# First attention of a two-layer network: values and exponential sums gathered by halves of the queries in one PSUM bank, with the causal mask of the maxima added on VectorE

## The chip, the cores and the metric

One of the cores of a Trainium2 chip runs the whole network. The metric is the device time of one execution in microseconds (us). A core has five engines with a queue each: PE (TensorE, matrix multiplication), ACT (ScalarE), DVE (VectorE), POOL (GpSimd) and SP (SyncE, here the issuer of DMAs). They wait for each other by semaphores.

## What is computed

The program is two transformer layers. Only the first attention is touched. For each of 2 batches and 16 heads it computes, over 2048 tokens, two causal softmaxes and their difference on shared values of 32 columns:

```python
A1 = jnp.einsum('bhqd,bhkd->bhqk', Q1, K1) * scaling
A2 = jnp.einsum('bhqd,bhkd->bhqk', Q2, K2) * scaling
A1 = jnp.where(causal, A1, neg_inf)
A2 = jnp.where(causal, A2, neg_inf)
attn = jax.nn.softmax(A1, -1) - lam * jax.nn.softmax(A2, -1)
O = jnp.einsum('bhqk,bhkd->bhqd', attn, V)
```

The kernel keeps apart, for each of the two softmaxes (index `a`), the products of the exponentials with the values and the sums of the exponentials; both are stored, and the stage that follows (`attention0_out`) divides and subtracts.

## The kernel before

`attention0` handles the 32 heads (2 x 16) one after another. A head has 2048 queries in 4 tiles of 512 (`tq`, also called turns), and for tile `tq` the keys come in 4(tq+1) blocks of 128 (`kb`). That gives 40 steps `k` a head (`STEPS`), each with two halves, a = 0 and 1. In the last four steps of a turn, the diagonal ones, only the queries from `left(k)` = 0, 128, 256 or 384 on have keys to see, and all instructions are shortened to them.

What one step does:

- PE `score` (L768): scores, keys on partitions, 512 queries as columns, in bf16 (each number is split in three bf16 parts that are stacked along the contraction, with the negative maxima as three more rows). In a diagonal step a second matmul adds the mask (L772). There are three PSUM buffers `ps_s` (`RING_S`), so half-step n needs the exponential of half-step n-3.
- ACT (L683): the exponential, from `ps_s` to `probs`, a ring of 8 steps.
- PE `values` (L791), once for two steps: four matmuls in f32 with 32 output rows each, one per column strip of the array: step k and step k+1, each with a = 0 and 1, up to 512 columns. The profile counts each as two MATMULs, so eight make a group. Even and odd steps are thus added up in different strips of the one bank `ps_o`.
- POOL (L638): adds the exponentials of the odd step to those of the even one.
- PE `ones` (L809), once for four steps (`QUAD`): four f32 matmuls against ones, for the two added pairs and a = 0 and 1, into the bank `ps_l`.
- At the first turn of a head a matmul with zeros clears each of the two banks (L777).

Behind each turn ACT copies the odd and the even strips of `ps_o` (L655, L656) two steps into the next turn, and `ps_l` (L665) in its fifth step, DVE adds the odd to the even half (L734), and SP stores both results (`store`, two DMAs).

The maxima that the exponentials subtract are found a head ahead: for the next head, 80 products of 128 queries by up to 512 keys (`MAXIMA`; PE L820, three PSUM buffers `ps_m`), reduced by DVE (L708). In 32 of the 80 a block of 128 x 128 lies on the diagonal, and PE adds the mask to it by one more matmul (L823). They are spread over steps 2 to 31 of the head by a rule of proportion (`maxima_at`), 5 to 7 for two steps; steps 32 to 39, 0 and 1 have none. Then `turn_maxima` (L831) transposes the maxima, DVE splits them in three parts, and three DMAs write them into the stack of the next head. The first head's maxima stand alone at the start.

The order on PE is written out by hand in `step`, for every two steps k, k+1: score(k+2, 0), score(k+2, 1), a third of the maxima, score(k+3, 0), values(k), a second third, score(k+3, 1), the last third, and for each k that is a multiple of 4 `ones` of the four steps before. An engine waits in its own order; what stands behind a waiting instruction waits too. Behind a semaphore wait for `max_used`, for instance, stand the scores that ACT needs next.

## Time and profile before

| | us |
|---|---|
| median of 3 runs | 4359.77 |
| lowest, highest | 4359.03, 4366.46 |
| the profiled execution | 4362.48 |
| its span | 4360.6 |

The span runs from the first to the last instruction that the profile shows. The attention's steady part, from the first to the last transposition of maxima (L831), takes 346.5 to 2586.1 us. In the profile PE is the matmul side of TensorE, PEld the loading of weights beside it. A duration of a matmul there is its latency from start to end; matmuls of a stretch overlap, so what one costs is the distance from its start to the start of the next. PEclk is the share of TensorE's full clock (2.4 GHz) that was granted; half of it is 1.2 GHz.

### The profile page before, as it was taken

The numbers are of one execution on the slowest core, as the hardware profiler recorded it, in microseconds if no ns is written. First come the engines' busy times: TensorE is split into PE (matmuls) and PEld (weight loads), VectorE is DVE, ScalarE is ACT, GpSimd is POOL, SyncE is SP. The second block draws the span as 40 slices with busy tenths as digits, with TensorE's granted clock in tenths as the row PEclk, the third lists the DMA queues.
The fourth block names the chain that finished last, engine by engine and source line by source line (L and its number), as shares of the span: only waits on it lengthen the run. The fifth ranks groups of instructions, "written<-read, shape, count | busy, mean of one in ns | idle before, by whom it ended". The sixth has DMA issues, their size and how long they took to land. (4 is left out here: it accounts for less than half of the span.)

```text
span 4360.6 us, 69689 instructions
## 1 busy us (share of the span) xinstructions
PE 3700.6 (85%) x21166; PEld 1647.8 (38%) x21231; DVE 2467.0 (57%) x4628; ACT 1754.4 (40%) x3522; POOL 1706.6 (39%) x1117
## 2 busy tenths in 40 slices
PE   6869999999999999999999996753899678896794
PEld 3322333232323232323233323642455445555462
DVE  4456766575757576767676753767211276666102
ACT  2324665666656566666666663110122141111110
POOL 1313555555555555555555554400344231110203
PEclk9978999999999999999999997855899899996897
DMA  4431111111111111111111103210443200001332
GB/s 156 154 120 33 34 37 33 34 35 35 35 35 35 35 35 35 35 36 34 38 33 38 31 9 96 82 40 0 121 91 76 45 24 4 0 0 39 111 111 87
DMA packets 202326, 224.92 MB, mean 52 GB/s; under 512 B 86673, under 2 KB 162706, under 8 KB 195858
## 3 DMA queue, kind: packets, MB, share of 16 engines
q1 hardware_dynamic: 186642, 195.39, 15.3%
q0 software_dynamic: 15360, 25.44, 3.1%
q8 instruction: 175, 2.87, 0.3%
q14 instruction: 149, 1.22, 0.1%
HBM read 139.12 MB, written 80.87 MB: 50 GB/s over the span
## 5 line engine op out<-in xcount | busy, mean ns | idle before, releaser
L638 POOL TENSOR_TENSOR attention_probs<-attention_probs 128x1024 f32<-128x1024 f32 (+2 forms) x640 | 1228.1, 1921 | 1160.2 <-PE attention_ps_o L791 1160.1
L708 DVE TENSOR_REDUCE attention_chunk_max<-attention_ps_m 128x1 f32<-128x512 f32 (+3 forms) x2560 | 1394.2, 604 | 457.4 <-PE attention_ps_m L823 280.6
L683 ACT ACTIVATE attention_probs<-attention_ps_s 128x512 f32<-128x512 f32 (+3 forms) x2560 | 1199.5, 532 | 826.9 <-PE attention_ps_s L772 459.7
L768 PE MATMUL attention_ps_s<-attention_q_stack,attention_k_stack 99*128 99x512 bf16 (+3 forms) x2560 | 821.6, 354 | 91.1 <-ACT attention_probs L683 70.1
L820 PE MATMUL attention_ps_m<-attention_k_stack,attention_q_stack 96*128 96x512 bf16 (+3 forms) x2560 | 772.5, 357 | 48.7 <-DMA attention_v_head<-v_rows 34.5
L791 PE MATMUL attention_ps_o<-attention_probs,attention_v_head 128*32 128x512 f32 (+3 forms) x5120 | 647.4, 558 | 8.6 <-issue 5.0
L768 PEld LDWEIGHTS attention_ps_s<-attention_q_stack,attention_k_stack 99*128 99x128 bf16 x2560 | 234.0, 98 | 668.4 <-ACT attention_probs L683 466.0
L820 PEld LDWEIGHTS attention_ps_m<-attention_k_stack,attention_q_stack 96*128 96x128 bf16 x2560 | 224.9, 97 | 628.7 <-DVE attention_chunk_max L708 490.2
L809 PE MATMUL attention_ps_l<-attention_probs,consts 128*32 128x512 f32 (+1 forms) x2560 | 352.6, 580 | 9.7 <-POOL attention_probs L638 1.0
L734 DVE TENSOR_TENSOR attention_out_sb<-attention_even_sb,attention_odd_sb 64x512 f32<-64x512 f32 x128 | 115.0, 898 | 296.8 <-ACT attention_even_sb L656 290.9
L823 PE MATMUL attention_ps_m<-mask_q_bf,ident_bf 128*128 128x128 bf16 x1024 | 225.5, 223 | 0.0
L772 PE MATMUL attention_ps_s<-mask_k_bf,ident_bf 128*128 128x128 bf16 x1024 | 225.4, 226 | 0.0
L1602 DVE TENSOR_TENSOR experts_hidT<-experts_ps_b,experts_silu 128x512 f32<-128x512 f32 x64 | 44.3, 692 | 236.4 <-ACT experts_silu L1568 236.4
L791 PEld LDWEIGHTS attention_ps_o<-attention_probs,attention_v_head 128*32 128x32 f32 x5120 | 101.9, 109 | 181.9 <-issue 115.8
L1549 POOL DMA_INDIRECT experts_sum<-experts_y_sb,experts_index x64 | 100.8, 1574 | 143.6 <-ACT experts_y_sb L1576 128.9
L383 POOL TENSOR_TENSOR project_parts<-project_rest,project_parts 128x512 bf16<-128x512 f32 x64 | 73.7, 1157 | 192.5 <-ACT project_parts L368 192.4
L2252 DVE TENSOR_SCALAR experts_hidT<-experts_ps_a 128x512 f32<-128x512 f32 x32 | 22.1, 692 | 212.5 <-PE experts_ps_a L2270 212.5
L1985 PE MATMUL linear_ps_a<-linear_qblk,linear_kc 128*128 128x512 f32 x256 | 125.1, 615 | 12.4 <-DVE linear_qblk L1960 7.6
L1888 POOL TENSOR_TENSOR x<-x,linear_y 128x256 f32 (+1 forms) x32 | 24.7, 773 | 275.2 <-DVE linear_y L1946 275.2
L443 PE MATMUL project_ps_o<-project_hT,project_wqkv 128*128 128x512 f32 x256 | 113.7, 602 | 13.0 <-ACT project_hT L357 13.0
L1638 PE MATMUL experts_ps_y<-experts_w,experts_hidT 128*128 128x256 f32 x512 | 114.7, 382 | 10.4 <-DVE experts_hidT L1602 10.4
L1621 PE MATMUL experts_ps_a<-experts_xT,experts_w 128*128 128x512 f32 x256 | 122.0, 599 | 1.4 <-ACT experts_xT L1571 1.4
(283 smaller groups left out, 4108.8 us busy)
## 6 DMA issues: line engine op xcount, KB each, us to landing
qk_parts<-project_parts SPq DMA_DIRECT2D x64, 384.0 KB, 3.0
heads_out<-attention_out_sb SPq DMA_DIRECT2D x128, 128.0 KB, 2.3
out_heads<-heads_out SPq DMA_DIRECT2D x8, 2048.0 KB, 8.2
experts_w<-in_f_w SPq DMA_DIRECT2D x16, 1024.0 KB, 8.3
attention_q_stack<-qk_parts SPq DMA_DIRECT2D x32, 384.0 KB
attention_k_stack<-qk_parts SPq DMA_DIRECT2D x32, 384.0 KB
experts_w<-in_e_w SPq DMA_DIRECT2D x24, 512.0 KB, 4.8
v_rows<-project_v SPq DMA_DIRECT2D x8, 1024.0 KB, 4.2
```

The lines of the kernel that those rows point to most:

```text
L638: pool.tensor_tensor(probs[:, to, :, lo:], probs[:, to, :, lo:], probs[:, k % RING_P, :, lo:], ALU.add).then_inc(pair_ok, 1)
L683: act.activation(probs[:, k % RING_P, a, left(k):], ps_s[(2 * k + a) % RING_S][:, left(k):], ACT.Exp, scale=float(DH) ** -0.5).then_inc(pr ...
L708: last = dve.tensor_reduce(chunk_max[:, a, jq, c:c + 1], ps_m[m % RING_M][:, 0:width(m)], AX.X, ALU.max)
L734: dve.tensor_tensor(out[:, slot], even[:, slot], odd[:, slot], ALU.add).then_inc(out_ok, 1)
L768: last = pe.matmul(psum[:, lo:], ks[at][0:WITH_MAX, a, kb * P:(kb + 1) * P], qs[at][0:WITH_MAX, a, tq * GROUP + lo:(tq + 1) * GROUP], star ...
L772: last = pe.matmul(psum[:, lo:lo + P], core.ident_bf[:], core.mask_k_bf[:], start=False, stop=True)
L791: last = pe.matmul(ps_o[strip:strip + DV, lo:], vh[at][:, kb + n], probs[:, (k + n) % RING_P, a, lo:], start=tq > 0 and kb == 0, stop=kb = ...
L809: last = pe.matmul(ps_l[strip:strip + DV, left(k):], core.c("ones")[:, 0:DV], probs[:, k % RING_P, a, left(k):], start=tq > 0 and kb == 0, ...
L820: last = pe.matmul(ps_m[m % RING_M][:, 0:w], qs[at][0:STACK, a, jq * P:(jq + 1) * P], ks[at][0:STACK, a, c * GROUP:c * GROUP + w], start=T ...
L823: last = pe.matmul(ps_m[m % RING_M][:, w - P:w], core.ident_bf[:], core.mask_q_bf[:], start=False, stop=True)
L1621: last = pe.matmul(psum[:], w_up[n][now.at][:, k, m * P:(m + 1) * P], xT[now.part][:, k], start=(k == 0), stop=(k == DC - 1))
L1985: last = pe.matmul(ps_a[hg][:, 4 * n:4 * n + 4].rearrange("p h t -> p (h t)"), kc[1 - at][:, hg], qblk[:, hg, 4 * n:4 * n + 4].rearrange(" ...
```

## The change

- The strips of the array are given out anew. Two of the four strips take the even blocks of 128 queries and two the odd ones (`halves`), each for a = 0 and 1. So `values` is called for each step, with four matmuls of up to 256 columns, and all key blocks add up in the same place. `ones` is called for each pair, in the same form, and its sums go to the other half of the same bank. A bank holds 2 x 2 x 128 columns, values and sums; there are two such banks, `ps_o0` and `ps_o1`, used in turn. No clearing is needed, and no adding of halves.
- ACT makes one copy a turn (`take`, L651 of the changed kernel) in place of three, between the two exponentials of the new turn's fourth step; the semaphores `o_taken`, `l_taken` and `out_ok` give way to one, `taken`.
- SP stores a turn by four DMAs in place of two, with runs of 128 queries (512 bytes) in place of 512; the sums have 2 rows a head in memory in place of 4, and the next stage transposes them with the identity matrix in place of `fold`.
- The mask of the maxima leaves PE. DVE handles the 32 diagonal products a head by `tensor_tensor_reduce` (add `mask_wide`, then the maximum), which is built as two instructions, and the other 48 as before.
- The order on PE is rewritten: the first third of the maxima now stands between score(k+2, 0) and score(k+2, 1), the second third between score(k+2, 1) and score(k+3, 0), then values(k), values(k+1) and ones of the pair before in one block, then score(k+3, 1) and the last third.

```diff
             def take(head, turn):
                 slot = turn % RING_O
...
+                act.wait_ge(values_ok, head * N_STEPS + LAST[turn] + 1)
+                act.wait_ge(ones_ok, head * PAIRS + (LAST[turn] + 1) // PAIR + RING_P // PAIR)
+                act.activation(results[:, slot], ps_o[slot][:], ACT.Copy).then_inc(taken, 1)
...
                     w, to = width(m), chunk_max[:, a, jq, c:c + 1]
+                    if c == jq // GT:
+                        wait_apart(dve, max_ok, after * N_MAX + m + 1, core.passed)
+                        last = dve.tensor_tensor_reduce(ps_m[m % RING_M][:, 0:w], ps_m[m % RING_M][:, 0:w],
+                                                        mask_wide[:, GROUP - w:], 1.0, -3.0e38, ALU.add, ALU.max, to)
+                    else:
+                        dve.wait_ge(max_ok, after * N_MAX + m + 1)
+                        last = dve.tensor_reduce(to, ps_m[m % RING_M][:, 0:w], AX.X, ALU.max)
...
+            def strips(k):
+
+                first = left(k) // P
+                for half in range(2):
+                    block = (first - half + 1) // 2
+                    if block < BLOCKS:
+                        for a in range(2):
+                            yield (half * 2 + a) * DV, half, a, block
...
+                for strip, half, a, block in strips(k):
+                    last = pe.matmul(psum[strip:strip + DV, 0, block:], vh[at][:, kb], halves(k, a, half, block),
+                                     start=kb == 0, stop=False, tile_position=(0, strip), skip_group_check=True)
+                last.then_inc(values_ok, 1)
...
                     if more:
                         score(head, at, k + 2, 0)
+                        maxima(after, other, items[:third])
                         score(head, at, k + 2, 1)
-
-                    third = -(-len(items) // 3)
-                    maxima(after, other, items[:third])
-                    if more:
+                        maxima(after, other, items[third:2 * third])
                         score(head, at, k + 3, 0)
...
                     values(head, at, k)
+                    values(head, at, k + 1)
+                    if k > 0:
+                        ones(head, k // PAIR - 1)
+                    elif not is_first(head):
+                        ones(head - 1, PAIRS - 1)
+                    if more:
+                        score(head, at, k + 3, 1)
```

PE before, one pair of steps in the middle of a head (from a score to the first matmul of `ones`; L768 scores, L820 maxima, L823 their mask, L791 values, L809 ones):

```order
L768 MATMUL attention0_ps_s1<-attention0_q_stack0,attention0_k_stack0 128x512 [waits attention0_prob_ok]
L820 MATMUL attention0_ps_m1<-attention0_k_stack1,attention0_q_stack1 128x512 [waits attention0_max_used]
L820 MATMUL attention0_ps_m2<-attention0_k_stack1,attention0_q_stack1 128x256 [waits attention0_max_used]
L823 MATMUL attention0_ps_m2<-mask_q_bf,ident_bf 128x128
L768 MATMUL attention0_ps_s2<-attention0_q_stack0,attention0_k_stack0 128x512 [waits attention0_prob_ok]
L791 MATMUL attention0_ps_o<-attention0_probs,attention0_v_head0 32x512 [waits attention0_prob_ok]
L791 MATMUL attention0_ps_o<-attention0_probs,attention0_v_head0 32x512 x3
L820 MATMUL attention0_ps_m0<-attention0_k_stack1,attention0_q_stack1 128x512 [waits attention0_max_used]
L820 MATMUL attention0_ps_m1<-attention0_k_stack1,attention0_q_stack1 128x512 [waits attention0_max_used]
L768 MATMUL attention0_ps_s0<-attention0_q_stack0,attention0_k_stack0 128x512 [waits attention0_prob_ok]
L820 MATMUL attention0_ps_m2<-attention0_k_stack1,attention0_q_stack1 128x512 [waits attention0_max_used]
L809 MATMUL attention0_ps_l<-attention0_probs,consts 32x512 [waits attention0_l_taken,attention0_pair_ok]
```

PE in the changed kernel, the like place (L741 scores, L791 maxima, L770 values, L781 ones):

```order
L791 MATMUL attention0_ps_m2<-attention0_k_stack1,attention0_q_stack1 128x512 [waits attention0_max_used]
L741 MATMUL attention0_ps_s1<-attention0_q_stack0,attention0_k_stack0 128x512 [waits attention0_prob_ok]
L791 MATMUL attention0_ps_m0<-attention0_k_stack1,attention0_q_stack1 128x384 [waits attention0_max_used]
L791 MATMUL attention0_ps_m1<-attention0_k_stack1,attention0_q_stack1 128x512 [waits attention0_max_used]
L741 MATMUL attention0_ps_s2<-attention0_q_stack0,attention0_k_stack0 128x512 [waits attention0_prob_ok]
L791 MATMUL attention0_ps_m2<-attention0_k_stack1,attention0_q_stack1 128x512 [waits attention0_max_used]
L791 MATMUL attention0_ps_m0<-attention0_k_stack1,attention0_q_stack1 128x512 [waits attention0_max_used]
L741 MATMUL attention0_ps_s0<-attention0_q_stack0,attention0_k_stack0 128x512 [waits attention0_prob_ok]
L770 MATMUL attention0_ps_o1<-attention0_probs,attention0_v_head0 32x256 [waits attention0_prob_ok]
L770 MATMUL attention0_ps_o1<-attention0_probs,attention0_v_head0 32x256 x7
L781 MATMUL attention0_ps_o1<-attention0_probs,consts 32x256 [waits attention0_pair_ok]
L781 MATMUL attention0_ps_o1<-attention0_probs,consts 32x256 x3
```

Values and ones, which stood apart with maxima on both sides, are one block of 12 calls (24 MATMULs in a profile), and four of a pair's five maxima stand ahead of it, in one run that only scores interrupt.

ACT before, the first steps of a new turn (L683 exponentials, L655 and L656 the copies of the values):

```order
L683 ACTIVATE attention_probs<-attention_ps_s 128x512 [waits attention0_ones_ok]
L679 REGISTER_ALU
L683 ACTIVATE attention_probs<-attention_ps_s 128x512 [waits attention0_score_ok]
L653 REGISTER_ALU
L654 ISA [waits attention0_out_ok]
L655 ACTIVATE attention_odd_sb<-attention_ps_o 64x512 [waits attention0_values_ok]
L656 ACTIVATE attention_even_sb<-attention_ps_o 64x512
L679 REGISTER_ALU
L683 ACTIVATE attention_probs<-attention_ps_s 128x512 [waits attention0_score_ok]
```

ACT in the changed kernel, the fourth step of a new turn (L666 exponentials, L651 the copy):

```order
L666 ACTIVATE attention_probs<-attention_ps_s 128x512 [waits attention0_ones_ok]
L662 REGISTER_ALU
L666 ACTIVATE attention_probs<-attention_ps_s 128x512 [waits attention0_score_ok]
L662 REGISTER_ALU
L666 ACTIVATE attention_probs<-attention_ps_s 128x512 [waits attention0_score_ok]
L648 ISA
L649 ISA [waits attention0_stored0]
L650 REGISTER_ALU [waits attention0_values_ok]
L651 ACTIVATE attention_results_sb<-attention_ps_o 128x512 [waits attention0_ones_ok]
L662 REGISTER_ALU
L666 ACTIVATE attention_probs<-attention_ps_s 128x512 [waits attention0_score_ok]
```

The copies stood behind the second exponential of a turn and ahead of the third; the one copy stands behind the seventh.

## Rows read from the trace of the kernel before

**Rows 1.** The page, its parts 1 and 2 (40 equal slices of the span).

```profile
PE 3700.6 (85%) x21166; PEld 1647.8 (38%) x21231; DVE 2467.0 (57%) x4628; ACT 1754.4 (40%) x3522; POOL 1706.6 (39%) x1117
...
PEclk9978999999999999999999997855899899996897
```

**Rows 2.** Uses of one line, L831: one transposition for each of 32 heads.

```profile
L831 PE MATMUL attention_ps_m<-consts,attention_neg_max x32: 284/284/396, 346.5 to 2586.1; 128*32 128x128 f32 x32
```

**Rows 3.** Groups by line, 346.5 to 2586.1 us: name, count, busy us, mean ns.

```profile
L823 PE MATMUL attention_ps_m<-mask_q_bf,ident_bf 128*128 128x128 bf16 x992 | 215.5, 220 | 0.0
L734 DVE TENSOR_TENSOR attention_out_sb<-attention_even_sb,attention_odd_sb 64x512 f32<-64x512 f32 x123 | 111.5, 907 | 231.8 <-ACT attention_even_sb L656 225.8 <-DMA heads_out<-attention_out_sb 5.9
```

**Rows 4.** Timeline, middle of a head: start us, us taken, engine, instruction.

```profile
1971.22 4.46 DVE L708 TENSOR_REDUCE attention_chunk_max<-attention_ps_m 128x1 f32<-128x512 f32 x8
...
1972.55 0.39 PE L820 MATMUL attention_ps_m<-attention_k_stack,attention_q_stack 96*128 96x512 bf16 x1 [0.18 <-DVE attention_chunk_max L708]
...
1973.15 0.23 PE L820 MATMUL attention_ps_m<-attention_k_stack,attention_q_stack 96*128 96x128 bf16 x1
...
1973.22 0.22 PE L823 MATMUL attention_ps_m<-mask_q_bf,ident_bf 128*128 128x128 bf16 x1
...
1973.28 0.76 PE L768 MATMUL attention_ps_s<-attention_q_stack,attention_k_stack 99*128 99x512 bf16 x2
...
1974.57 0.38 PE L768 MATMUL attention_ps_s<-attention_q_stack,attention_k_stack 99*128 99x512 bf16 x1
...
1974.88 1.06 PE L791 MATMUL attention_ps_o<-attention_probs,attention_v_head 128*32 128x512 f32 x8
...
1975.88 0.50 PE L820 MATMUL attention_ps_m<-attention_k_stack,attention_q_stack 96*128 96x512 bf16 x2
...
1976.06 2.36 POOL L638 TENSOR_TENSOR attention_probs<-attention_probs 128x1024 f32<-128x1024 f32 x1 [3.38 <-PE attention_ps_o L791]
...
1976.31 1.62 DVE L708 TENSOR_REDUCE attention_chunk_max<-attention_ps_m 128x1 f32<-128x512 f32 x3 [0.63 <-PE attention_ps_m L820]
```

**Rows 5.** Timeline of PE where one head ends and the next begins.

```profile
1946.87 0.63 PE L791 MATMUL attention_ps_o<-attention_probs,attention_v_head 128*32 128x256 f32 x8
...
1947.88 0.22 PE L772 MATMUL attention_ps_s<-mask_k_bf,ident_bf 128*128 128x128 bf16 x1
1950.44 0.49 PE L768 MATMUL attention_ps_s<-attention_q_stack,attention_k_stack 99*128 99x384 bf16 x1 [2.35 <-issue]
...
1952.38 1.65 PE L791 MATMUL attention_ps_o<-attention_probs,attention_v_head 128*32 128x512 f32 x8 [0.36 <-issue]
```

**Rows 6.** Timeline of ACT at the same place.

```profile
1947.83 1.08 ACT L683 ACTIVATE attention_probs<-attention_ps_s 128x512 f32<-128x512 f32 x2 [2.57 <-PE attention_ps_s L772]
1948.93 0.59 ACT L655 ACTIVATE attention_odd_sb<-attention_ps_o 64x512 f32<-64x512 f32 x1
1949.54 0.59 ACT L656 ACTIVATE attention_even_sb<-attention_ps_o 64x512 f32<-64x512 f32 x1
```

**Rows 7.** Stretches there: us, busy us (count) by engine, PEclk, DMA share, GB/s.

```profile
1946.40:1950.40 4.00, 1.60 (x14) 0.54 (x14) 0.12 (x1) 2.54 (x5) 1.10 (x2) 0.98 0.20 43
1950.40:1953.80 3.40, 3.00 (x16) 1.08 (x17) 0.56 (x1) 1.36 (x5) 0.00 (x0) 0.53 0.32 90
```

**Rows 8.** DVE's groups by shape, whole span.

```profile
L708 DVE TENSOR_REDUCE attention_chunk_max<-attention_ps_m 128x1 f32<-128x512 f32 x1792 | 1150.9, 683 | 219.3 <-PE attention_ps_m L820 168.3 <-PE attention_ps_m L823 42.5
L708 DVE TENSOR_REDUCE attention_chunk_max<-attention_ps_m 128x1 f32<-128x128 f32 x256 | 73.3, 286 | 195.0 <-PE attention_ps_m L823 195.0
L1757 DVE TENSOR_SCALAR project_low<-project_ps_o,project_bias 128x512 f32<-128x512 f32 x32 | 23.8, 745 | 25.5 <-PE project_ps_o L1789 25.5
L1936 DVE TENSOR_TENSOR linear_state<-linear_ps_s,consts 128x512 f32<-128x512 f32 x32 | 22.1, 692 | 48.7 <-PE linear_ps_s L2007 48.7
L1951 DVE TENSOR_SCALAR linear_den<-linear_ps_tok 128x16 f32<-128x16 f32 x32 | 5.3, 165 | 0.0
```

**Rows 9.** A stretch of the later linear attention, columns as in rows 7.

```profile
3622.31:3624.02 1.71, 1.71 (x28) 1.06 (x28) 1.71 (x2) 0.00 (x0) 0.00 (x0) 1.00 0.00 0
```

More of the change, by code:

```diff
@@ L779, in values @@
             def values(head, at, k):
                 turn, tq, kb = STEPS[k]
[L782 removed]
+                psum = ps_o[turn % RING_O]
+                if kb % PAIR == 0:
+                    pe.wait_ge(prob_ok, head * 2 * N_STEPS + 2 * k + 4)
                 if kb == 0:
[L785 to L793 removed]
@@ L794, in values @@
[L794 to L811 removed]
+                    pe.wait_ge(taken, head * Q_TILES + turn + 1)
@@ L879, in step @@
                 if after is None:
-                    ones(head, QUADS - 1)
+                    ones(head, PAIRS - 1)
             run(pe, step)
```

174 lines of the change are left out of this document (57 added, 117 removed).

## The prediction

> **What bounds the kernel now.** First the busy shares and the slices [rows 1]: PE is the engine with most work. Then one line that runs once a head [rows 2]: from 346.5 to 2586.1 us there are 31 heads, so a head takes 2239.6 / 31 = 72.25 us. That period is what the change touches.
>
> A PE duration is a latency, not a price, so I price by distances between starts [rows 4]. A mask matmul lasts 0.22 us, but starts at 1973.22 with the next start at 1973.28: it costs 0.06. A group of eight values matmuls starts at 1974.88, and the next matmul at 1975.88: 1.00 us, of which 4 x 512 columns at 2.4 GHz are 0.85. The score ahead of it started at 1974.57 and has 0.21 us of columns, so 0.10 goes in front of the group too. A change from full-array to strip matmuls and back thus costs 0.10 + 0.15 = about 0.24 us a group.
>
> By such prices PE's work a head is: scores and maxima 34,816 columns each, 14.8 us each with a few ns a matmul; 64 masks 3.8; values 16 x 0.85 + 4 x 0.43 = 15.4; ones 10 x 0.85 = 8.5; 30 changes 7.2; two clearings and the transposition about 0.6. Sum 65.1 us. The other 7.2 us of the period are PE's waits and slow clock, and two places hold nearly all of it.
>
> The first is the seam between heads [rows 5, 6]. After 1947.88 PE issues nothing until 1950.44, 2.6 us, since the score that stands next needs an exponential that ACT runs behind two copies (1948.93 and 1949.54). Right behind that hole the granted clock is 0.53 for 3.4 us [rows 7], that is mostly the 1.2 GHz level, where before it was 0.98. This costs about 1.7 us. From the last group of values of one head to the second of the next, holes and slow clock come to some 3.9 us of the 7.2.
>
> The second is where DVE falls behind with the maxima: reduces of 512 columns back to back, eight in 4.46 us, and PE issuing one product per 0.60 us (1972.55, 1973.15), waiting for DVE [rows 4]. Sevens of maxima in two steps occur twice a head; such places sum to about 2.6 us. Short waits in the steps that have no maxima make the rest.
>
> **The change, part by part, in us a head.** *Removed from PE's work.* 32 masks x 0.06 = 1.9. Twenty blocks in place of thirty groups: 10 x 0.24 = 2.4. Ones in the last two steps of a turn need half the columns they did: 4 x 0.21 = 0.85. Clearings 0.45. Together -5.6. The columns of values don't change: four strips of 512 for two steps became twice four strips of 256. Between the six quarters of a block I take nothing, since within a group the trace shows the 0.85 of columns and only one 0.15 beside it [rows 4]; the bound above is 0.03 for each of four more joints in 20 blocks, +2.4.
>
> *The seam.* The copies leave the place where PE waits for them. What stays is ACT's own chain: from the end of the last block six scores (1.2 us of PE) go with exponentials of 512, 384 and 384 columns; by the delay of 0.4 from a matmul to its reader and about 0.5 and 0.4 us an exponential, the first block of the new head starts 2.1 us later. That leaves 0.8 us of waits in short pieces, and 0.5 for the last exponential of the old head and POOL's sum. No hole is left like the one ahead of the slow clock, so I take the clock to stay up. Seam: 3.9 becomes 1.4, -2.5.
>
> *Steps without maxima.* Before, ones stood between two scores and filled the time of an exponential in every other pair. Now nothing stands there: a score, 0.4 to its exponential, 0.6 until the third score behind it may start, 1.0 in all, against 0.65 of scores. 0.2 to 0.4 in each of four pairs, +0.4 net.
>
> *DVE's price.* A diagonal maximum is now two instructions. The main one has a row near it, an addition from PSUM of 512 columns, 692 ns against 683 for a reduce [rows 8]. For the second, a column of result, the bound below is a reduce's fixed share: 683 at 512 columns and 286 at 128 leave about 0.15 of duration at none, and as back-to-back reduces start 0.60 apart with 0.68 of duration, 0.07 of spacing. The bound above is 0.165, the whole duration of a 16-column operation, and 0.06 for operands (745 against 683). So a diagonal one costs 0.08 to 0.23 more; a gain is excluded, as the columns are the same and an instruction comes on top. I take 0.12, nearer the lower row, since small operations overlap. On DVE: +3.8, and -4 x 0.9 for the additions of halves that go [rows 3]: level.
>
> *PE's wait for DVE.* This is the term that decides. The chain by rows 4: product to reduce 0.43 (1975.88 to 1976.31), reduce to reduce 0.60, and from a reduce's start to the product that gets its buffer 0.73 (1971.22 + 0.60 = 1971.82, the product at 1972.55). In the new order a usual pair puts on PE, from 0: score, m1, m2, score, m3, m4 (which would start at 1.15), score, then the block of 1.5, score, m5. The m5 of the pair before started at -0.22; its reduce starts at 0.20, that of m1 at 0.80, and m4 can start at 0.80 + 0.73 = 1.53. So PE waits 0.4 us at m4, and 0.06 at m3; behind m4 stand the score that ACT needs and the block. Later DVE is idle through the end of the block. In the old order the values group (1.1 us) lay between the second and third product, and gave DVE the time. For the 15 pairs with maxima: thirteen at 0.1 to 0.8 (mostly 0.5), and the two sevens at 1.2, come to 8.9, against 2.6 now: +6.3. The dearer diagonal ones (0.12 where the chain was followed with 0.085) add 0.4.
>
> *Others.* Four stores for two a turn lie on SP and the DMA queues, with 0.2 to 0.3 DMA share at most there [rows 7]: nothing. POOL's addition (2.36, rows 4) must end within one pair's time instead of two; pairs take 3.4 and more with maxima, 2.6 to 2.8 without, and a block reaches its ones 0.9 after its start, so this is hidden, with 0.3 counted at the seam. The first head's maxima stand alone and are DVE's: 32 x 0.12 = +4 once.
>
> **Sum.** -5.6 - 2.5 + 0.4 + 6.3 + 0.4 = -1.0 a head; 31 heads -31, +4 at the start: -27. Profiled execution 4362.5 - 27 = 4335.5; the median of the runs is 2.7 lower, so 4333.
>
> **Rivals.** *DVE's waits are small.* If bursts of products cost half of what the chain says, +6.3 becomes +2: 4.3 a head, -133 more, 4200. For it: before, PE waits little in most pairs. Against it: 0.73 and 0.60 are measured, and the order leaves only three buffers for five products. Chance 0.17.
>
> *Slower by the price on DVE.* If the pair of instructions costs over 0.22 more than a reduce, the waits grow by about 1 us a head for each 0.1. The place is m1 to m4 in every pair. At 0.30 it is +1.9 a head against my 0.12: +57, 4390. The deciding point is near 0.20. Chance 0.15.
>
> *Slower by the clock.* If the remaining waits at the seam still bring a slow stretch, its 1.7 us a head comes back: +52, 4386. For it: most slices of PEclk show 9 in place of 10 [rows 1], so slow stretches recur. Against it: behind 1.0 us waits elsewhere [rows 4] the clock stayed up. Chance 0.15.
>
> *Slower by the issue of small matmuls.* A block has 24 matmuls and as many weight loads in 1.3 us, 0.054 us each. The densest stretch of the trace has 28 in 1.71, 0.061 each, of which some began earlier [rows 9]; a run of 24 there takes about 1.6. If PE can't issue faster, blocks are 0.2 to 0.3 longer, 20 x 0.25 = +5 a head, minus what it hides of DVE's wait: about +110, 4445. The Trainium skill, "TensorE: Matmul & The Clock Gate", section "Wait — 56ns, not 53.3ns?", says that without hardware decoding the sequencer spends about 62 ns on each MATMUL, which binds below that. By this estimate a block of 24 would take 1.49, +0.2 x 20 = 4 a head. That section also gives a 25 ns floor, by which nothing is lost. The eight of a values group within 0.85 don't test it. Chance 0.08.
>
> **How the numbers follow.** Forecast case 0.43, at 4333 with 4290 to 4370 of its own; the last 0.02 is anything else. What this kernel's measurement can tell from no change is about 0.2%, 9 us. The forecast case gives 0.31 faster, 0.09 same, 0.03 slower; small waits 0.17 faster; the two at 4390 give 0.25 slower and 0.05 same; issue 0.08 slower. Faster 0.49, same 0.14, slower 0.37. The range leaves out half of each outer case: 4200 to 4430.
>
> **What would show it.** L831's first and last start should give 71.2 us a head. Each pair should show a wait of PE for DVE of about 0.4 at the fourth maximum, blocks of 24 matmuls 1.3 to 1.5 long, DVE's two instructions with 0.12 more spacing than a reduce, no 2.6 us hole at the seam and PEclk 1.00 through it. The prediction is wrong if the joints within a block cost time, if the clock drops in new places where DVE's waits have thinned PE's work, or if the second DVE instruction waits for the first to drain.

## The result, and the profile of the changed kernel

| | before | changed |
|---|---|---|
| median, us | 4359.4 (4 runs) | 4482.78 (4 runs) |
| lowest, highest | 4355.14, 4366.46 | 4474.97, 4493.79 |
| profiled execution, its span | 4362.48, 4360.6 | 4480.47, 4478.3 |

The ratio is 1.0283, 95% interval 1.0257 to 1.0309: the change costs 123 us, 2.8%. The forecast was 4333, with 4200 to 4430 as its range; the time lies above both, and the sign was wrong.

The period of a head is read where it was read before [rows 2], by the line that runs once a head:

```profile
L798 PE MATMUL attention_ps_m<-consts,attention_neg_max x32: 275/275/397, 352.1 to 2707.8; 128*32 128x128 f32 x32
```

A head takes (2707.8 - 352.1) / 31 = 75.99 us, where it took 72.25 and 71.2 was forecast. That is 116 of the 118 us between the two profiled executions. So the whole loss lies in the attention's steady part. The page's first part agrees: PE is busy for less time than before [rows 1], in a longer span.

```profile
PE 3670.1 (82%) x27309; PEld 1875.8 (42%) x27311; DVE 2402.8 (54%) x5524; ACT 1663.4 (37%) x3266; POOL 1704.2 (38%) x1117
```

PE therefore waits more. For whom is in its list of waits (352 to 2707 us: what waited for what, us in total, times, longest); the like list of the kernel before stands first.

```profile
PE attention_ps_s L768 <- ACT attention_probs L683: 63.5, 114, 2.5
...
PE attention_ps_m L820 <- DVE attention_chunk_max L708: 9.2, 33, 3.3
PE attention_ps_s L768 <- issue: 7.3, 3, 2.5
```

```profile
PE attention_ps_m L791 <- DVE attention_chunk_max L696: 79.0, 304, 0.4
PE attention_ps_s L741 <- ACT attention_probs L666: 67.9, 77, 5.5
PE attention_ps_m L791 <- DVE attention_chunk_max L692: 37.4, 124, 0.4
PE attention_ps_s L741 <- issue: 28.2, 8, 3.9
```

Two things are new: waits for DVE, 9.2 before and 116.4 now, and single waits for ACT of up to 5.5 us. This list counts only time in which PE is empty; since a matmul's record is longer than its share of the array, short waits hide in it. So for the rest of the text I also use an account by distances between starts: over the whole steady part, the distance from each matmul to the next, less its columns at 2.4 GHz and 5 ns, is put down to the matmul that came late. In us a head:

| kernel | period | scores and maxima, columns | values and ones | late maxima | late scores, under 1.5 us | late scores, over 1.5 us |
|---|---|---|---|---|---|---|
| before | 72.25 | 33.55 | 29.24 | 1.65 | 3.00 | 0.82 |
| changed | 75.99 | 31.69 | 27.39 | 9.37 | 2.08 | 3.12 |

"Values and ones" holds the whole distance from each of these matmuls to the next start. A change from scores to strips is outside these columns (about 0.1 each, 30 before and 20 now), and so are smaller items.

**Late maxima.** Timeline of PE and of DVE in the middle of a head, columns as in [rows 4]:

```profile
1536.76 0.38 PE L741 MATMUL attention_ps_s<-attention_q_stack,attention_k_stack 99*128 99x512 bf16 x1
...
1537.08 0.23 PE L791 MATMUL attention_ps_m<-attention_k_stack,attention_q_stack 96*128 96x128 bf16 x1
1537.73 0.39 PE L791 MATMUL attention_ps_m<-attention_k_stack,attention_q_stack 96*128 96x512 bf16 x1 [0.42 <-DVE attention_chunk_max L692]
...
1538.27 1.07 PE L770 MATMUL attention_ps_o<-attention_probs,attention_v_head 128*32 128x256 f32 x16
1539.16 0.61 PE L781 MATMUL attention_ps_o<-attention_probs,consts 128*32 128x256 f32 x8
1539.70 0.34 PE L741 MATMUL attention_ps_s<-attention_q_stack,attention_k_stack 99*128 99x384 bf16 x1
```

```profile
1536.89 0.72 DVE L692 CUSTOM_DVE_ANT_0 attention_ps_m<-attention_ps_m,attention_mask_wide 128x512 f32<-128x512 f32 x1
1537.53 0.14 DVE L692 DVE_READ_ACCUMULATOR2_ANT attention_chunk_max<- 128x1 f32 x1
1537.53 0.69 DVE L696 TENSOR_REDUCE attention_chunk_max<-attention_ps_m 128x1 f32<-128x512 f32 x1
1538.13 0.29 DVE L692 CUSTOM_DVE_ANT_0 attention_ps_m<-attention_ps_m,attention_mask_wide 128x128 f32<-128x128 f32 x1
1538.34 0.14 DVE L692 DVE_READ_ACCUMULATOR2_ANT attention_chunk_max<- 128x1 f32 x1
1538.34 0.69 DVE L696 TENSOR_REDUCE attention_chunk_max<-attention_ps_m 128x1 f32<-128x512 f32 x1
...
1540.40 0.43 DVE L692 CUSTOM_DVE_ANT_0 attention_ps_m<-attention_ps_m,attention_mask_wide 128x256 f32<-128x256 f32 x1 [1.38 <-PE attention_ps_m L791]
```

The fourth maximum of the pair, at 1537.73, is 0.42 late, and the score and the block stand behind it. Then comes the block, 1.43 us from 1538.27 to 1539.70, and DVE runs dry within it: 1.38 us idle before 1540.40. That is the wait of which the prediction spoke, at its place and of its size. Over all pairs of steps, the eleven with five maxima a head are 0.41 late at the fourth and 0.11 at the third, and the two with seven lose 1.2 each. The same rows show two more things. The read of the accumulator starts together with the next instruction (1537.53 both times), so it takes no time of its own on DVE. From start to start, where DVE is never idle, the median is 0.607 us for a pair of 512 columns and 0.598 for a reduce, 0.207 and 0.198 for 128 columns: 0.01 more (single distances reach 0.65 with both). And a block of 24 matmuls takes 3072 columns at 2.4 GHz, 1.28, and 0.15.

**Late scores.** In 22 of the 31 heads ACT, then PE, stops. SP's row (DMA issues: start, how long the issue took), the ACT copy and the PE behind it:

```profile
1498.03 2.15 SPq L577 DMA_DIRECT2D attention_q_stack<-qk_parts  x3
1500.37 1.97 SPq L577 DMA_DIRECT2D attention_k_stack<-qk_parts  x3
1502.53 0.41 SPq L580 DMA_DIRECT2D attention_v_head<-v_rows  x1
1503.27 20.40 SPq L611 DMA_DIRECT2D heads_out<-attention_results_sb  x1
1523.88 0.60 SPq L613 DMA_DIRECT2D exp_sums<-attention_results_sb  x1
```

```profile
1526.14 0.39 PE L791 MATMUL attention_ps_m<-attention_k_stack,attention_q_stack 96*128 96x512 bf16 x1 [0.26 <-DVE attention_chunk_max L696]
...
1527.33 0.60 ACT L651 ACTIVATE attention_results_sb<-attention_ps_o 128x512 f32<-128x512 f32 x1 [3.69 <-DMA exp_sums<-attention_results_sb]
...
1528.46 0.40 PE L741 MATMUL attention_ps_s<-attention_q_stack,attention_k_stack 99*128 99x512 bf16 x1 [1.94 <-ACT attention_probs L666]
```

The first of the four stores of a turn is issued right behind the next head's seven loads and takes SP 20.40 us; the other three follow from 1523.88. The result buffer of that turn is wanted again two turns later, so ACT's copy waits 3.69 us for it, and behind the copy stand the exponentials. In the eight heads behind a loop's edge (below) the hold was 16.1 to 18.2 us, and only one copy waited, 0.91 us. The copies waited for `exp_sums` 22 times, 92.1 us in all. Before, the same store was held too. SP's row in the kernel before, then ACT's waits for the store behind it (346.5 to 2586.1 us):

```profile
1519.74 20.79 SPq L617 DMA_DIRECT2D heads_out<-attention_out_sb  x1
```

```profile
ACT attention_total_sb L665 <- DMA exp_sums<-attention_total_sb: 9.1, 5, 2.7
```

The held buffers were those of DVE's addition of halves, which waited 5.9 us in all [rows 3] with nothing urgent behind it, and of ACT's copy of the sums, which waited 9.1 us. So ACT was tied to the hold before as well, but it waited only five times.

Behind 20 of the 22 waits of the copy, PE ran at the 1.2 GHz level for 3.4 or 6.8 us; behind a wait for DVE it did not. Stretches, columns as in [rows 7]: behind the stop at 1528.46, and across DVE's waits at 1518 to 1521.5.

```profile
1528.40:1531.90 3.50, 3.44 (x26) 1.20 (x27) 0.00 (x0) 1.48 (x4) 1.06 (x1) 0.54 0.17 39
1518.00:1521.50 3.50, 3.02 (x29) 1.33 (x29) 3.00 (x7) 1.44 (x3) 0.72 (x1) 1.00 0.15 56
```

**The seam.** The hole where one head ends and the next begins [rows 5] is still there, and longer, but only at every third head:

```profile
1574.03 0.22 PE L745 MATMUL attention_ps_s<-mask_k_bf,ident_bf 128*128 128x128 bf16 x1
1577.59 0.50 PE L741 MATMUL attention_ps_s<-attention_q_stack,attention_k_stack 99*128 99x384 bf16 x1 [3.34 <-issue]
```

At the head after it the same instructions run without a stop:

```profile
1651.37 0.39 PE L741 MATMUL attention_ps_s<-attention_q_stack,attention_k_stack 99*128 99x512 bf16 x1
...
1651.88 0.33 PE L741 MATMUL attention_ps_s<-attention_q_stack,attention_k_stack 99*128 99x384 bf16 x1
...
1653.49 0.85 PE L770 MATMUL attention_ps_o<-attention_probs,attention_v_head 128*32 128x256 f32 x14
```

The stretch from the first of the seam's six scores to the first values of the new head takes 2.12 us here, just the 2.1 of the prediction. And the kernel before has the same two kinds, told apart by which head one looks at. An ordinary seam of before:

```profile
1804.40 0.39 PE L768 MATMUL attention_ps_s<-attention_q_stack,attention_k_stack 99*128 99x512 bf16 x1
...
1804.91 0.33 PE L768 MATMUL attention_ps_s<-attention_q_stack,attention_k_stack 99*128 99x384 bf16 x1
...
1807.13 0.28 PE L768 MATMUL attention_ps_s<-attention_q_stack,attention_k_stack 99*128 99x256 bf16 x1 [1.25 <-ACT attention_probs L683]
...
1807.94 1.05 PE L791 MATMUL attention_ps_o<-attention_probs,attention_v_head 128*32 128x512 f32 x8
```

The score at 1804.91 is the one that started at 1950.44 in [rows 5], and nothing holds it. ACT beside it:

```profile
1805.50 0.59 ACT L655 ACTIVATE attention_odd_sb<-attention_ps_o 64x512 f32<-64x512 f32 x1
1806.11 0.59 ACT L656 ACTIVATE attention_even_sb<-attention_ps_o 64x512 f32<-64x512 f32 x1
```

What the two copies cost PE is the 1.25 at 1807.13. Over all seams the stretch takes 3.64 us before and 2.16 now at the 23 ordinary ones, 5.02 and 5.63 at the other 8. The 8 lie three heads apart (637, 860, 1077, 1296, 1514, 1732, 1948 and 2163 us before), and the loop over heads, `run`, has three heads in a round.

### The profile page after: what moved, and what is told of

It is laid out like the page before. It is cut to its first block and busy times, and to the rows that moved or that the text cites. A ratio compares the mean times of both kernels' runs of the same rounds, so it can differ in the third digit from the quotient of the medians.

```text
span 4478.3 us, 84226 instructions
## 1 busy us (share of the span) xinstructions
PE 3670.1 (82%) x27309; PEld 1875.8 (42%) x27311; DVE 2402.8 (54%) x5524; ACT 1663.4 (37%) x3266; POOL 1704.2 (38%) x1117
## 3 DMA queue, kind: packets, MB, share of 16 engines
q14 instruction: 168, 1.38, 0.1%
## 5 line engine op out<-in xcount | busy, mean ns | idle before, releaser
L666 ACT ACTIVATE attention_probs<-attention_ps_s 128x512 f32<-128x512 f32 (+3 forms) x2560 | 1247.9, 536 | 997.6 <-PE attention_ps_s L741 517.8
L696 DVE TENSOR_REDUCE attention_chunk_max<-attention_ps_m 128x1 f32<-128x512 f32 x1536 | 998.9, 685 | 368.2 <-PE attention_ps_m L791 368.2
L791 PE MATMUL attention_ps_m<-attention_k_stack,attention_q_stack 96*128 96x512 bf16 (+3 forms) x2560 | 837.5, 361 | 177.5 <-DVE attention_chunk_max L696 80.7
L741 PE MATMUL attention_ps_s<-attention_q_stack,attention_k_stack 99*128 99x512 bf16 (+3 forms) x2560 | 880.2, 358 | 122.3 <-ACT attention_probs L666 72.7
L692 DVE CUSTOM_DVE_ANT_0 attention_ps_m<-attention_ps_m,attention_mask_wide 128x128 f32<-128x128 f32 (+3 forms) x1024 | 496.9, 498 | 508.6 <-PE attention_ps_m L791 505.5
L770 PE MATMUL attention_ps_o<-attention_probs,attention_v_head 128*32 128x256 f32 (+1 forms) x9728 | 655.1, 374 | 0.4 <-ACT attention_probs L666 0.4
L791 PEld LDWEIGHTS attention_ps_m<-attention_k_stack,attention_q_stack 96*128 96x128 bf16 x2560 | 246.6, 98 | 616.5 <-DVE attention_chunk_max L696 329.1
L741 PEld LDWEIGHTS attention_ps_s<-attention_q_stack,attention_k_stack 99*128 99x128 bf16 x2560 | 248.3, 98 | 546.2 <-ACT attention_probs L666 224.0
L781 PE MATMUL attention_ps_o<-attention_probs,consts 128*32 128x256 f32 (+1 forms) x5120 | 422.3, 368 | 2.4 <-POOL attention_probs L633 1.2
L770 PEld LDWEIGHTS attention_ps_o<-attention_probs,attention_v_head 128*32 128x32 f32 x9728 | 267.0, 111 | 267.7 <-issue 107.6
L781 PEld LDWEIGHTS attention_ps_o<-attention_probs,consts 128*32 128x32 f32 x5120 | 192.2, 112 | 104.4 <-POOL attention_probs L633 33.1
L692 DVE DVE_READ_ACCUMULATOR2_ANT attention_chunk_max<- 128x1 f32 x1024 | 144.6, 141 | 0.0
L651 ACT ACTIVATE attention_results_sb<-attention_ps_o 128x512 f32<-128x512 f32 x128 | 76.4, 597 | 179.3 <-DMA exp_sums<-attention_results_sb 92.1
```

The lines of the kernel that those rows point to most:

```text
L666: act.activation(probs[:, k % RING_P, a, left(k):], ps_s[(2 * k + a) % RING_S][:, left(k):], ACT.Exp, scale=float(DH) ** -0.5).then_inc(pr ...
L692: last = dve.tensor_tensor_reduce(ps_m[m % RING_M][:, 0:w], ps_m[m % RING_M][:, 0:w], mask_wide[:, GROUP - w:], 1.0, -3.0e38, ALU.add, ALU ...
L696: last = dve.tensor_reduce(to, ps_m[m % RING_M][:, 0:w], AX.X, ALU.max)
L741: last = pe.matmul(psum[:, lo:], ks[at][0:WITH_MAX, a, kb * P:(kb + 1) * P], qs[at][0:WITH_MAX, a, tq * GROUP + lo:(tq + 1) * GROUP], star ...
L770: last = pe.matmul(psum[strip:strip + DV, 0, block:], vh[at][:, kb], halves(k, a, half, block), start=kb == 0, stop=False, tile_position=( ...
L781: last = pe.matmul(psum[strip:strip + DV, 1, block:], core.c("ones")[:, 0:DV], halves(k, a, half, block), start=False, stop=kb == GT * (tq ...
```

## Experiments

All are compared with runs of the kernel before on the same chip (4366.34, 4364.31 and 4365.65 us for the three groups of runs below). "Changed" stands for 4482.78, measured where the kernel before took 4359.4; so a difference from it is less sure than a ratio, and by the ratios the gains over the changed kernel would be 5 to 7 us larger. The account by distances between starts, us a head:

| kernel | time | period | values and ones | late maxima | late scores, short | late scores, over 1.5 us |
|---|---|---|---|---|---|---|
| changed | 4482.78 | 75.99 | 27.39 | 9.37 | 2.08 | 3.12 |
| four result buffers | 4386.68 | 73.01 | 26.68 | 9.25 | 1.86 | 1.26 |
| stores ahead of loads | 4383.33 | 72.99 | 26.59 | 9.27 | 1.93 | 1.26 |
| maxima spread | 4372.95 | 72.82 | 27.60 | 3.63 | 2.32 | 5.07 |
| thirds as before | 4415.56 | 73.86 | 27.63 | 5.56 | 2.29 | 4.28 |
| four buffers and spread | 4208.33 | 67.32 | 26.73 | 3.33 | 2.07 | 1.19 |
| that, six heads a round | 4177.61 | 66.38 | 26.54 | 3.29 | 2.18 | 0.43 |
| that of 4208, mask on PE | 4240.21 | 68.35 | 26.74 | 2.32 | 1.76 | 1.71 |

**Four result buffers.** The wait of the copy is taken away by buffers:

```diff
-        results = s.sb("results_sb", [P, RING_O, 2, BLOCKS, P], F32)
+        results = s.sb("results_sb", [P, Q_TILES, 2, BLOCKS, P], F32)
-        stored = [s.sem(f"stored{i}") for i in range(RING_O)]
+        stored = [s.sem(f"stored{i}") for i in range(Q_TILES)]
...
-                act.activation(results[:, slot], ps_o[slot][:], ACT.Copy).then_inc(taken, 1)
+                act.wait_ge(stored[turn], (head + 1) * (STORES * 16))
+                act.activation(results[:, turn], ps_o[turn % RING_O][:], ACT.Copy).then_inc(taken, 1)
```

> The changed kernel with four buffers for a turn's results in place of two, so that a copy on ACT waits for the store of the same turn one head earlier. Theory S (stores): once a head ACT's copy waits 4 us for a store that SP issues late (92 us in 22 waits), PE stands still 2.3 to 4.5 us behind it, and a slow clock follows; this goes: 2.5 to 3 us a head, 75 to 95 us, 4385 to 4410. Rival D (DVE alone): all that matters is PE's wait for DVE, and what the stores hold up is made good later: within 15 us of the changed kernel's 4483.

Measured: 4386.68 us (4379.43 to 4395.21), ratio to before 1.0046 (1.003 to 1.0063), 96 us under the changed kernel. ACT's waits for `exp_sums` are gone from its list, and of the late scores over 1.5 us the eight holes at the loop's edge make up most of what is left. So a term that the prediction put at nothing costs 96 us, 3.0 of every head.

**Stores ahead of loads.** Is it the place of the store in the queue, or are four stores of 512-byte runs too slow? Two buffers again, one edit on SP:

```diff
+                if head is not None and not is_first(head.n):
+                    store(head.n, 0)
                 if later is not None:
...
                     load(later)
                 for turn in range(Q_TILES):
-                    if head is not None and not (is_first(head.n) and turn == 0):
+                    if head is not None and turn > 0:
                         store(head.n, turn)
```

> The changed kernel with one edit on SP: the two turns' order at a head's start is turned round, so that the four stores of the turn that ended last are issued ahead of the next head's seven loads, not behind them. Two result buffers as in the changed kernel, same maxima order. Theory S (the long wait of ACT's copy once a head comes from a store that stands behind loads in the DMA queue and holds SP 20 us): the stores of the first turn now land at once, the 20 us fall on the next turn's first store, whose buffer is not wanted until half a head later; ACT's waits for exp_sums go from 92 us to under 5, and the time is that of four result buffers, 4387 (4378 to 4396), about -95 against the changed kernel. Rival D (it is the number or the 512-byte runs of the stores, not their place): the waits stay, 4460 to 4485. Rival B (four buffers helped by something else than this wait): in between, 4410 to 4450.

Measured: 4383.33 us (4382.37 to 4389.31), ratio 1.0046 (1.0028 to 1.0063). SP's row:

```profile
1532.74 0.71 SPq L613 DMA_DIRECT2D heads_out<-attention_results_sb  x1
...
1535.33 0.56 SPq L615 DMA_DIRECT2D exp_sums<-attention_results_sb  x1
1536.42 2.17 SPq L577 DMA_DIRECT2D attention_q_stack<-qk_parts  x3
1538.82 2.04 SPq L577 DMA_DIRECT2D attention_k_stack<-qk_parts  x3
1541.07 0.41 SPq L580 DMA_DIRECT2D attention_v_head<-v_rows  x1
1541.84 21.80 SPq L613 DMA_DIRECT2D heads_out<-attention_results_sb  x1
```

The same four stores are issued in 3.2 us when they stand ahead of the loads. The hold of 21.80 us is still there, on whatever store comes first behind the loads; it now falls on one whose buffer isn't wanted for half a head. The number of stores is not the cause, their place is. Why a store behind loads is held, no run shows.

**Maxima spread.** Two fifths of a pair's maxima stay ahead of the block, the rest go behind it; never more than one between two scores ahead of it:

```diff
-                        maxima(after, other, items[:third])
                         score(head, at, k + 2, 1)
-                        maxima(after, other, items[third:2 * third])
+                        maxima(after, other, items[:split])
                         score(head, at, k + 3, 0)
+                        maxima(after, other, items[split:ahead])
...
+                    maxima(after, other, behind[:len(behind) - close])
                     if more:
                         score(head, at, k + 3, 1)
...
-                    maxima(after, other, items[2 * third:])
+                    maxima(after, other, behind[len(behind) - close:])
```

> The changed kernel with the maxima of a pair of steps in other places on PE and nothing else: three of five behind the block (two, a score, one), two ahead of it, one before and one after its last score. Theory D: the fourth maximum no longer comes before its buffer is free; PE's waits ahead of maxima fall from 9.4 to 2 to 3 us a head, time 4483 - 31 x 7 = 4265, 4240 to 4300. Rival A (ACT): the scores wait for exponentials instead, as soon as the maxima don't; then the gain is under 2 us a head, 4420 or more.

Measured: 4372.95 us (4362.06 to 4381.49), ratio 1.0009 (0.9992 to 1.0027), 110 us under the changed kernel: neither the 4265 of theory D nor the 4420 of its rival. Late maxima fall from 9.37 to 3.63 a head, 5.7 x 31 = 178 us, but the stops of the copy grow with it: its waits for `exp_sums` go from 92.1 us to

```profile
ACT attention_results_sb L651 <- DMA exp_sums<-attention_results_sb: 145.4, 29, 9.6
```

A faster head comes sooner to a buffer that becomes free at the same time.

**Thirds as before.** The maxima placed against scores and values as in the kernel before, with the block kept (one third between the second and third score, one behind the block, one at the end).

```diff
-                        maxima(after, other, items[:third])
                         score(head, at, k + 2, 1)
-                        maxima(after, other, items[third:2 * third])
+                        maxima(after, other, items[:third])
                         score(head, at, k + 3, 0)
...
+                    maxima(after, other, items[third:2 * third])
```

> The changed kernel with the thirds of the maxima where the kernel before had them against scores and values: one behind the second score, one behind the block, one behind the fourth score. Theory D by its chain: five maxima still come in one run between two blocks of 1.5 us, and the fifth waits for the buffer of the second, 0.45 us as now; so this alone brings little, 4450 to 4500. Rival (order of thirds is the cause): the time falls by the growth of that wait, 7 us a head, to about 4265.

Measured: 4415.56 us (4412.18 to 4421.01), ratio 1.0104 (1.0074 to 1.0134), 67 us under the changed kernel. I had expected next to no gain here, since the block puts four maxima close together behind it instead of ahead of it. Late maxima fell to 5.56. A likely reason, not followed further, is that behind the block DVE has caught up and all three buffers are free, so that only what comes fourth in a row waits; no run shows it. Late scores over 1.5 us grew at the same time, from 3.12 to 4.28, which hides part of the gain.

**Four buffers and spread.** Both edits together.

> Four result buffers and the spread maxima together. If both theories hold the gains add up: 4483 - 85 - 217 = 4180, under both kernels. If the waits share a cause or cover each other, it stays within 30 us of the better of the two alone.

Measured: 4208.33 us (4202.94 to 4213.34), ratio 0.9629 (0.96 to 0.9658): 274 us under the changed kernel and 158 under the one before, near the 4180 at which the gains add up. The two single gains add to 206; the other 68 are nearly all the stops of the copy that the spread alone had brought back: four buffers take 1.86 us a head of late scores from the changed kernel and 3.88 from the spread one, a difference of 62 us. With both causes gone the rest of the change (new strips, one copy a turn, another order) is a clear gain.

**The mask, three times.** The kernel before with only the mask of the maxima on DVE; the changed kernel with the mask on PE again; the kernel of 4208 us with the mask on PE again. The edit, in the first of them:

```diff
-                    dve.wait_ge(max_ok, after * N_MAX + m + 1)
-                    last = dve.tensor_reduce(chunk_max[:, a, jq, c:c + 1], ps_m[m % RING_M][:, 0:width(m)], AX.X,
-                                             ALU.max)
+                    if c == jq // GT:
+                        wait_apart(dve, max_ok, after * N_MAX + m + 1, core.passed)
+                        last = dve.tensor_tensor_reduce(ps_m[m % RING_M][:, 0:w], ps_m[m % RING_M][:, 0:w],
+                                                        mask_wide[:, GROUP - w:], 1.0, -3.0e38, ALU.add, ALU.max, to)
...
-                    diagonal = c == jq // GT
+                    diagonal = False
```

> The kernel before with one part of the change alone: DVE adds the mask of the 32 diagonal maxima a head by its pair of instructions, PE doesn't. In the changed kernel's trace the pair is spaced as one reduce (0.21 us at 128 columns, 0.60 at 512), so theory M (the mask is worth its 0.058 us a matmul): PE's work falls by 1.9 us a head, 4366 - 58 = 4308, 4295 to 4330. Rival: where PE saves, it waits for DVE instead: 4350 or more.

> The changed kernel with this one part undone: PE adds the mask, DVE reduces only. Theory D: the mask matmuls lie among the run of maxima that waits for DVE anyway, so part of their 1.9 us a head is covered: 4483 + 0 to 35. Rival: additive, 4483 + 58 = 4541. That DVE's pair of instructions costs much would show as a faster kernel: under 4470.

> Spread maxima and four result buffers (4208), with the mask on PE again. Here PE hardly waits for DVE, so theory M says the whole 1.9 us a head shows: 4208 + 58 = 4266, 4245 to 4275. Rival: the matmuls fall in waits that are left (3.3 us a head ahead of maxima): within 25 us of 4208.

Measured: 4331.43 us (ratio 0.9929, 0.9913 to 0.9946), 33 under the kernel before; 4482.29 (1.0266, 1.0248 to 1.0284), the same as the changed kernel; 4240.21 (0.9713, 0.9697 to 0.973), 32 over the one with the mask on DVE. The second is where theory D had it; the first lies just above theory M's 4330 and the third between the two forecasts, so neither theory nor rival holds there. The matmuls saved are 1.86 us a head in all three, 58 us. Where PE waits for DVE anyway, the saved time only lengthens the wait: with the mask on PE late maxima are 7.50 in place of 9.37, and nothing is gained. Where it hardly waits, somewhat over half of the 58 is kept; late maxima are 3.33 with the mask on DVE and 2.32 with it on PE, which takes 1.0 of the 1.86, and in the kernel before they are 2.66 and 1.65, the same 1.0. The pair costs DVE 0.01 us more than a reduce, 0.3 a head, so I read most of this as PE coming sooner to a buffer that DVE has not freed; no run separates the two.

**Six heads in a round.** The hardware loop of `run` with twice the body, in the kernel of 4208 us and in the kernel before:

```diff
-            with engine.Fori(0, rounds) as i:
-                for n in range(1, 1 + STACKS):
-                    heads(i, n, 3)
-            for n in range(1 + STACKS * rounds, HEADS):
+            with engine.Fori(0, rounds // 2) as i:
+                for n in range(1, 1 + 2 * STACKS):
+                    heads(2 * i, n, 3)
+            for n in range(1 + STACKS * (rounds // 2 * 2), HEADS):
```

> Spread maxima and four result buffers, with six heads in one round of the hardware loop in place of three (4 rounds in place of 9, and 7 heads written out behind it in place of 4). In the traces PE stands still 3.7 to 4.2 us where a round begins anew, at every third head (2.5 to 2.7 in the kernel before), with no wait on another engine. Theory L: this belongs to the loop's edge and recurs only there; five edges fewer are worth 5 x 3.9 plus the slow clock behind some of them, 20 to 30 us: 4180 to 4190. Rival: it is the price of code that is loaded from memory anyhow, and more code costs as much elsewhere: within 8 us of 4208.

> The kernel before with one edit: the hardware loop over heads has six heads in a round in place of three, four rounds in place of nine or eight; no instruction of a head is changed. Theory L (the 2.6 us hole between two heads is the loop's edge, at every third head): the holes over 2 us in PE's row go from 8 to 3, five times 2.6 us and some of the slow clock behind them, 1 to 1.7 us each: -13 to -21 us, 4343 to 4352 where the kernel before has 4364. Rival C (the hole comes of ACT's two copies, as the prediction had it): nothing changes, 4360 to 4368, and 8 holes or more remain.

Measured: 4177.61 us (4177.34 to 4186.25; ratio 0.9571, 0.9555 to 0.9587), and 4352.39 (4346.67 to 4360.47; ratio 0.9965, 0.9953 to 0.9978): 31 and 13 us less, at the edges of the ranges that theory L gave. In both the holes over 2 us at the seams fall from 8 to 3, six heads apart. No instruction of a head was changed, and ACT's copies stand where they stood. So the hole of [rows 5] belongs to the loop's edge. One of the three that remain in the kernel before:

```profile
1295.51 0.22 PE L772 MATMUL attention_ps_s<-mask_k_bf,ident_bf 128*128 128x128 bf16 x1
1297.97 0.50 PE L768 MATMUL attention_ps_s<-attention_q_stack,attention_k_stack 99*128 99x384 bf16 x1 [2.24 <-ACT attention_probs L683]
```

Here the profile names ACT as the releaser, though the same score elsewhere has no wait: a name given to the end of a hole is not its cause. 4177.61 is the fastest kernel of this study, 4.3% under the one before.

## Why the prediction was wrong

Its own sum, per head, against what was measured. "Free" is the kernel with the stores ahead of the loads: the changed kernel without the stops of the copy.

| term | forecast | measured |
|---|---|---|
| PE's work | -5.6 | -1.9 (scores, maxima) and -3.6 (values, ones, with the changes of mode; "free") |
| seam, and steps without maxima | -2.5 + 0.4 | about -1.4 ("free"; what is left over) |
| late maxima | +6.3 + 0.4 | +7.6 ("free") |
| stores | 0 | +3.0 |
| sum | -1.0 | +3.7 |

**The step that failed is "Others": "Four stores for two a turn lie on SP and the DMA queues, with 0.2 to 0.3 DMA share at most there [rows 7]: nothing."** A share of bandwidth can't tell of a hold in issue order. The 20 us issue was in the trace of before, in SP's row, a row that the prediction did not use. The change tied a more urgent waiter to it: ACT's only copy of a turn, with the exponentials and so PE behind it, which waited 92.1 us where the copy of the sums had waited 9.1 and DVE's addition 5.9. The prediction moved each copy in its sum but asked only where the copy stands, not what it waits for; the order rows show `stored0` ahead of it. Two experiments, one by buffers and one by order, give 96 and 99 us. It is 3.0 of the 4.7 us a head by which the sum was wrong, and it decided that the time fell outside the range: without the hold it would be 4383 us.

**The term that "decides" was right, and its base was not.** 8.9 and 0.4 us of waits for DVE were forecast, 9.37 were measured, with 0.4 us at the fourth maximum of a pair and 1.2 in each pair with seven, as the chain had it. But the kernel before waited 1.65, not 2.6, so the difference is 7.7 in place of 6.7. The 9.3 also came out right partly by chance: the 0.12 for the second DVE instruction is 0.01 in the trace, and the lower bound of 0.08 was wrong too, since the read of the accumulator lies under the next instruction. The rival that put the waits at half is refuted, and so is the one with a dearer DVE pair.

**The seam was read wrong, though its sum was nearly right.** The prediction took the hole of 2.6 us for ACT's copies and counted it for every head. The row itself said "issue". The exponential behind the copies had not even ended when the score started at 1950.44, so the score did not wait for it:

```profile
1950.03 0.47 ACT L683 ACTIVATE attention_probs<-attention_ps_s 128x384 f32<-128x384 f32 x1
```

And the distances between such holes would have shown it at every third head only. The copies do cost PE time, 1.25 us in one wait further on, and moving them made the 23 ordinary seams 1.5 us shorter, to the 2.1 forecast. At the 8 edges the stretch became 0.6 us longer. The mean is -0.9; with the waits in front of values and ones that went, about -1.4 in place of -2.1.

**The clock.** The rival "the clock stays slow" was half true. The prediction expected 1.00 through the seam. In the kernel with the stores first, the clock's records show eight stretches at the 1.2 GHz level in the steady part, 41 us in all, one at each edge; in the kernel before, 28 stretches and 109 us, 19 of them at ordinary seams. In the changed kernel as it is, 28 stretches make 137 us, 8 at edges and 20 behind stops of the copy: what the ordinary seams gave back, the stops of the copy took. DVE's waits of 0.2 to 0.4 us brought none: with the stores first they are still 9.27 us a head, and no stretch lies away from an edge.

**Right**: a block of 24 matmuls takes 1.43 us, which is its columns and one entry and exit, so the four joints within it cost nothing and the rival of 4445 us by the issue of small matmuls is refuted. The shortest block of 24, whose eight matmuls for `ones` have 128 columns each:

```profile
1507.12 1.07 PE L770 MATMUL attention_ps_o<-attention_probs,attention_v_head 128*32 128x256 f32 x16
1508.00 0.40 PE L781 MATMUL attention_ps_o<-attention_probs,consts 128*32 128x128 f32 x8
1508.34 0.39 PE L741 MATMUL attention_ps_s<-attention_q_stack,attention_k_stack 99*128 99x512 bf16 x1
```

It takes 1.22 us, 0.051 each, and 1.22 is again its 2560 columns (1.07) and 0.15. Columns count here as the longest strip has them: blocks in which only two of four strips are shorter in the second step (2816 columns by the sum) take 1.43 or 1.44 like the full ones. The Trainium skill's figure of about 62 ns per MATMUL without hardware decoding ("TensorE: Matmul & The Clock Gate", "Wait — 56ns, not 53.3ns?") would give 1.49; the trace has 1.22, so that limit does not bind here. Whether the chip decodes in hardware here, no run shows.

Even with the stores free the changed kernel is at 4383, 0.5% slower than before. So the forecast "faster" would have been wrong by the base of the waits for DVE and the seam alone, though within its range.

## What to carry to other kernels

When a change moves a step to another engine or queue, list what the moved instruction waits for, and look up in the trace when each of these is done, on the row of the engine that issues it; here that was SP's row. A buffer that is freed by a DMA store is only as free as the issuing queue: put stores ahead of bulk loads, or give the results one buffer per turn. And before a hole is priced for every round of a loop, list all its occurrences: one that comes at every third head is the loop's, not the head's.

## What the hardware showed that I had not expected

- The read of the accumulator behind DVE's add-and-maximum costs no spacing; it lasts 0.14 us but starts with the next instruction (1537.53). Back to back, the pair takes 0.607 us for 512 columns and 0.207 for 128 (medians), a reduce 0.598 and 0.198.
- A store that is the first behind seven loads takes SP 16.1 to 25.5 us to issue, mostly 20 to 21 (after the first head; kernels before, changed, and stores first); the same stores ahead of the loads take 0.5 to 0.7 each.
- The edge of the hardware loop stops PE for 2.5 to 2.7 us in the kernel before and 3.6 to 4.1 in the changed one (from start to start), and a stretch at the 1.2 GHz level followed each. A longer body does not make it longer: with six heads a round it was 2.3 to 2.6 and 2.8 to 3.3. What sets its length stays open.
- Matmuls in strips of 256 columns follow each other without a gap in blocks of 24: 1.28 us of columns in 1.43. A strip that is shortened beside longer ones saves nothing (1.43 or 1.44 as well).
